# Swin block on one core: a new order of logits, max logits, value blocks and fc2 rows in the attention loop

## The chip, the cores and the metric

The kernel runs on one core of one Trainium2 chip. The metric is the time of one execution on the device, in microseconds (us). Before the change three runs gave 3938.79, 3946.13 and 3956.12 us, median 3946.13 us.

## What is computed

One Swin Transformer block on an image batch x of shape (32, 56, 56, 128), float32, 16 heads of 8 channels, windows of 7 x 7 = 49 tokens, shifted by 3:

```python
y = roll(layernorm(x) * norm1_g + norm1_b, (-3, -3))       # then cut into windows of 49 tokens
q, k, v = split_heads(y @ qkv_w.T + qkv_b)
attn = (q * HD ** -0.5) @ k.T + relative_bias + shift_mask  # 49 x 49 for each window and head
o = softmax(attn) @ v
x = x + roll_back(o @ proj_w.T + proj_b)
h = gelu((layernorm(x) * norm2_g + norm2_b) @ fc1_w.T + fc1_b)   # 512 hidden channels
out = x + h @ fc2_w.T + fc2_b
```

## The kernel before

The work is cut into 128 steps (`STEPS`). A step is a band of 7 image rows of two images: two times 8 windows. A "pair" is the same window of both images, so a step has 8 pairs, w = 0 to 7 (`NW`). One image's tokens lie on partitions 0 to 48 and the other's on 64 to 112. Everything is unrolled in Python: `turns(body)` (L188; each engine has its own `body(t, edge, odd)`) goes over t = -2 to 130, and in turn t an engine works on several steps at once. TensorE's turn t has the transposes, q/k projection and max logits of step t + 1, the logits, exponentials and value products of step t, the projection of step t - 1, fc1 and the last four fc2 rows of step t - 2, and the first three fc2 rows of step t - 3. The order inside a turn is written by hand, one program for each engine; semaphores alone join them. Each engine runs its own program strictly in order.

The softmax needs a maximum for each query and head ahead of the exponentials. It comes from a cheaper product, the "max logits" (high halves of q and k only), computed one turn before: `max_logits` (L743, matmuls L755, 8 for each pair) writes PSUM banks 0 and 1, VectorE's `row_maxima` (L588, reduction L592) takes the maxima, and since there is one such pair of banks, `max_logits` of pair w waits until the maxima of pair w - 1 are taken (`s_max`). For pair 0 it waits for the DMAs that bring its operands mx_k and mx_q (`s_mx_dma`, issued by SyncE at L278 and L282) and for x1 of an earlier step.

`logits` (L766) of pair w has 12 matmuls: the bias and mask by a selection matrix (L785) and q times k with the maximum folded in as a row (L790). It writes banks 2 and 3 for even w and 4 and 5 for odd w, so from w = 2 on it waits for the exponential of pair w - 2 (`s_exp`). ScalarE's `exp_pair` (L404, L411) reads them and writes `probs`, which has four buffers. `pv` (L794, L805) multiplies the probabilities of pairs 2u and 2u + 1 with the values, 64 matmuls into bank 6; it waits for both exponentials, and for ScalarE's copy (`copy_pv`, L414, L419) of the value block before it. ScalarE's order in the loop is exp 0, a copy of v, exp 1, exp 2, copy of block 0, exp 3, exp 4, copy of block 1, exp 5, exp 6, copy of block 2, exp 7; the copy of block 3 opens its next turn.

`fc2` (L823; L837 high parts, L842 low part, 12 matmuls) computes one of the seven image rows of the second MLP product into bank 7. Rows 3 to 6 stand in the attention loop (p = 1), rows 0 to 2 (p = 0) near the start of the turn. VectorE's `finish` (L566, L574) adds the residual; row 0 of the next group waits for it.

After the loop the next turn of TensorE begins with value block 3 (`pv(t - 1, NU - 1)`), the transposes of z2 (L858) and x_in (L866), the transposes of the maxima (L763), fc2 rows 0 to 2 of step t - 3, two chunks of fc1 (L819), the q/k projection (L887), two more chunks of fc1, the spread of the reciprocals (L901), v (L915) and the output projection (L924).

SyncE's queue issues nearly all DMAs, in a fixed order of its own in each turn: `sums` out of `pv_sb`, after the copy of value block 3 (L235, L237); `x_in` (L244, issued at L186), after the x transposes (L243); `oT_raw` (L250); the maxima (L226); `r_rows` (L263), after GpSimd's `r_lo` (L261, L367); the maxima again; `mx_k` (L278); `mx_q` (L282); the output; and the operands of the logits, `st_k` and `st_q` (L297, L300). GpSimd's `r_lo` comes out of VectorE's reciprocal of `sums` (L633).

Of the kernel before, what the change touches and what calls it, by code (L numbers as in the profile page):

```python
# [18 lines left out]
NW = W // WS  # L19
WT = WS * WS  # L20
BT = NW * WT
NU = NW // 2
# [14 lines left out]
EPS = 1e-5  # L37
HALVES = ((0, 4), (4, 7))
FC2_PARTS = ((0, 3), (3, 7))
HT = WS * TP // 2  # L40
W_SCALE = 64.0
LOW_SCALE = 2048.0
# [7 lines left out]
def swin_block_kernel(nc, x, wqT, wkT, wvT, wvpT, wpT, w1T, w2T, cols, rows, table_k, table_q, ident, eye,  # L50
# [11 lines left out]
    with ctx:  # L62
# [101 lines left out]
        def exists(n):  # L164
            return 0 <= n < STEPS

        def past(n, k):
            return n > k
# [332 lines left out]
        def _(dve):  # L501
# [64 lines left out]
            def finish(n, p, edge):  # L566

                i0, i1 = FC2_PARTS[p]
                if p == 1:
# [150 lines left out]
        def _(pe):  # L720
# [45 lines left out]
            def logits(n, w, edge, par):  # L766
                if w == 0:
                    pe.wait_ge(s_st_dma, N_ST * (n + 1))
                    pe.wait_ge(s_neg_dma, N_NEG * (n + 1))
                    if past(n, 1):  # L770
                        pe.wait_ge(s_gelu, CH * (n - 1) - 1)
                    elif n == 1:
                        pe.wait_ge(s_exp, NW - 1)
                elif w == 1:
                    if past(n, 1):
                        pe.wait_ge(s_gelu, CH * (n - 1))
                    elif n == 1:
                        pe.wait_ge(s_exp, NW)
                else:
                    pe.wait_ge(s_exp, NW * n + w - 1)  # L780
                kind = 2 * edge(n) + (w == NW - 1)
                bank = 2 + 2 * (w % 2)
                for b in range(2):
                    for im in range(2):
                        mm(ps[HP * im:HP * (im + 1), bank + b, 0:HB * WT], eye_k[0:BIAS_ROWS, kind, im, :],  # L785
                           bias[0:BIAS_ROWS, b, :], start=True, stop=False)
                    for g in (2 * b, 2 * b + 1):
                        for im in range(2):
                            span = slice((2 * w + im) * WT, (2 * w + im + 1) * WT)
                            last = mm(group(im, bank, g, EQ * WT), st_k[par][:, g, span], st_q[par][:, :, g, span],  # L790
                                      start=False, stop=(g % 2 == 1))
                last.then_inc(s_st, 1)

            def pv(n, u):  # L794
                pe.wait_ge(s_exp, NW * n + 2 * u + 2)
                if u == 0:
                    pe.wait_ge(s_vown, n + 1)
                    pe.wait_ge(s_vown_b, 3 * (n + 1))
                else:
                    pe.wait_ge(s_pv_sb, NU * n + u)  # L800
                for w in (2 * u, 2 * u + 1):
                    for h in range(NH):
                        g, r = h // NR, h % NR
                        first = (2 * g + w % 2) * WT
                        last = mm(ps[32 * r:32 * r + VC, 6, first:first + WT],  # L805
                                  v_own[0:KP, w, h, :], probs[0:KP, w % 4, h * WT:(h + 1) * WT], start=True, stop=True)
                last.then_inc(s_pv, 1)
# [15 lines left out]
            def fc2(n, p, i):  # L823
                first, end = FC2_PARTS[p]
                if i == first and p == 1:
# [18 lines left out]
                    last.then_inc(s_fc2, 1)  # L844

            def body(t, edge, odd):
                if exists(t - 1):
                    pv(t - 1, NU - 1)
                n = t - 2
                if exists(n):  # L850

                    pe.wait_ge(s_z2, n + 1)
                    if exists(t - 1):
                        pe.wait_ge(s_exp, NW * t - 1)
                    else:
                        pe.wait_ge(s_gelu, CH * n)
                    for i in range(WS):
                        last = nc.tensor.transpose(tokens_of(2)[:, i, 0:TP], z2[:, i, :], idn[0:TP, 0:TP])  # L858
                    last.then_inc(s_t2, 1)
                n = t + 1  # L860
                if exists(n):
                    pe.wait_ge(s_z1, n + 1)
                    if past(n, 0):
                        pe.wait_ge(s_max, NW * n)
                    for i in range(WS):
                        last = nc.tensor.transpose(tokens_of(0)[:, i, 0:TP], x_in[odd(1)][:, i, :], idn[0:TP, 0:TP])  # L866
                    last.then_inc(s_t1, 1)
                if exists(t):
                    max_transposed(t)
                if exists(t - 3):  # L870
                    for i in range(*FC2_PARTS[0]):
                        fc2(t - 3, 0, i)
                if exists(t - 2):
                    fc1(t - 2, 0)
                    fc1(t - 2, 1)
                n = t + 1
                if exists(n):
                    pe.wait_ge(s_y_lo, n + 1)
                    high, low = ([y[odd(1)][:, :, im, 0:WT] for im in range(2)] for y in (yT_hi, yT_lo))
                    for w_hi, w_lo, bank in ((wk_hi, wk_lo, 0), (wq_hi, wq_lo, 6)):  # L880
                        if bank == 6 and exists(t):
                            pe.wait_ge(s_negT, t + 1)
                        if bank == 6 and exists(t - 3):
                            pe.wait_ge(s_fin, 2 * (t - 3) + 2)
                        for k, (ww, yy) in enumerate(((w_hi, high), (w_hi, low), (w_lo, high))):
                            for im in range(2):
                                last = mm(ps[:, bank + im, 0:BT], ww[:, :], yy[im], start=(k == 0), stop=(k == 2))  # L887
                        last.then_inc(s_qk, 1)
                if exists(t - 2):
                    fc1(t - 2, 2)  # L890
                    fc1(t - 2, 3)
                n = t - 1
                if exists(n):

                    pe.wait_ge(s_rr_dma, N_RR * (n + 1))
                    if exists(t + 1):
                        pe.wait_ge(s_lo, 2 * (t + 1) + 1)
                    elif not exists(t):
                        pe.wait_ge(s_x1, 2 * n)
                    for b in range(2):  # L900
                        last = mm(tokens_of(0)[:, 4 * b:4 * b + 4, 0:2 * WT], sel[:, :], r_rows[:, 4 * b:4 * b + 4, :],  # L901
                                  start=True, stop=True)
                    last.then_inc(s_spread, 1)
                n = t
                if exists(n):
                    if exists(t + 1):
                        pe.wait_ge(s_lo, 2 * (t + 2))
                    else:
                        pe.wait_ge(s_negT, t + 1)
                        if exists(t - 3):  # L910
                            pe.wait_ge(s_fin, 2 * (t - 3) + 2)
                    for b in range(2):
                        for w in range(4 * b, 4 * b + 4):
                            for part, (yy, ww) in enumerate(((yT_hi, wv_hi), (yT_lo, wv_hi), (yT_hi, wv_lo))):
                                last = mm(ps[:, 7 - b, (w % 4) * C:(w % 4 + 1) * C],  # L915
                                          yy[odd(0)][:, w, :, :].rearrange("p m q -> p (m q)"), ww[:, :],
                                          start=(part == 0), stop=(part == 2))
                        last.then_inc(s_v, 1)
                n = t - 1
                if exists(n):  # L920
                    pe.wait_ge(s_oT, n + 1)
                    for i0, i1 in HALVES:
                        for i in range(i0, i1):
                            last = mm(tokens_of(0)[0:TP, i, :], oT[:, i, :], w_p[:, :], start=True, stop=True)  # L924
                        last.then_inc(s_proj, 1)
                for w in range(NW):
                    if exists(t):
                        if w != 1:
                            logits(t, w, edge, odd(0))
                        if w == 0:  # L930
                            logits(t, 1, edge, odd(0))
                        if w % 2 == 0 and w > 0:
                            pv(t, w // 2 - 1)
                    if exists(t - 2) and w % 2:
                        fc2(t - 2, 1, FC2_PARTS[1][0] + w // 2)
                    if exists(t + 1):
                        max_logits(t + 1, w, edge)

            turns(body)


# [60 lines left out]
```

## Time and profile before

| | before |
|---|---|
| median of three runs | 3946.13 us (3938.79 to 3956.12) |
| the profiled execution | 3954.99 us, span 3953.2 us, mean granted TensorE clock 0.996 |
| busy share of the span | PE 95%, PE weight loads 75%, DVE 78%, ACT 70%, POOL 73% |
| matmuls | 75664 |
| HBM traffic | 106.14 MB read, 51.46 MB written |

PE is TensorE, PEld its weight loads, DVE is VectorE, ACT ScalarE, POOL GpSimd, SP SyncE and SPq its DMA queue. A matmul's start is recorded; its end is modelled, and matmuls overlap, so that a distance from start to start says more than a duration. An idle time in the list of waits counts from the modelled end of the instruction before.

### The profile page before, as it was taken

To read this page: it belongs to the slowest core of one execution; us is meant where nothing else is said; L and a number is where in the kernel's file an instruction comes from. 1 tells how busy PE (TensorE), PEld (TensorE's weight loads), DVE (VectorE), ACT (ScalarE), POOL (GpSimd) and SP (SyncE) were. 2 spreads that over 40 slices of the span, in tenths; PEclk is the share of its full clock that TensorE was granted. 3 is DMA by queue.
4 is the path that set the end of the run, shared out by engine and by line. 5 is a ranking of instruction groups with operands and counts; after the bars stand their busy time and mean duration, and the time that the engine had idled before them with its cause. 6 is when DMAs were issued, how large, how long until landed. Compare 5 with 4: busy or idle time off the path is not lost. (4 is left out here: it accounts for less than half of the span.)

```text
span 3953.2 us, 177003 instructions
## 1 busy us (share of the span) xinstructions
PE 3758.8 (95%) x75664; PEld 2946.1 (75%) x75664; DVE 3089.6 (78%) x7840; ACT 2778.9 (70%) x3840; POOL 2895.7 (73%) x3988
## 2 busy tenths in 40 slices
PE   2899999999999999999999999999999999999997
PEld 1677777777777777777777777777777777777776
DVE  6787788788788778777778878878878877777774
ACT  1677777777777777777777777777777777776674
POOL 5577777777777777777777777777777777777775
PEclk9999999999999999999999999999999999999999
DMA  2333343333333433333434433343343343333331
GB/s 78 105 114 110 117 117 113 117 115 115 117 115 113 118 110 115 118 113 114 117 112 117 115 114 114 112 119 111 114 121 111 115 119 112 113 115 109 110 108 58
DMA packets 609604, 442.02 MB, mean 112 GB/s; under 512 B 142083, under 2 KB 608371, under 8 KB 608819
## 3 DMA queue, kind: packets, MB, share of 16 engines
q1 hardware_dynamic: 608355, 428.88, 36.7%
q8 instruction: 597, 9.78, 1.1%
q0 software_dynamic: 464, 1.81, 0.1%
q14 instruction: 188, 1.54, 0.1%
HBM read 106.14 MB, written 51.46 MB: 40 GB/s over the span
## 5 line engine op out<-in xcount | busy, mean ns | idle before, releaser
L592 DVE TENSOR_REDUCE neg_max<-ps 113x16 f32<-113x784 f32 x1024 | 999.9, 977 | 594.1 <-PE ps L755 443.7
L411 ACT ACTIVATE probs<-ps 113x784 f32<-113x784 f32 x1024 | 849.2, 829 | 704.4 <-PE ps L790 539.7
L380 POOL TENSOR_TENSOR hid_lo<-probs,hid_hi 128x784 f16<-128x784 f32 x512 | 881.6, 1744 | 75.2 <-DVE hid_hi L585 75.0
L790 PE MATMUL ps<-st_q,st_k 128*49 128x196 f16 x8192 | 695.0, 249 | 0.0
L785 PE MATMUL ps<-bias,eye_k 106*64 106x392 f16 x4096 | 684.7, 332 | 0.3 <-issue 0.3
L755 PE MATMUL ps<-mx_k,mx_q 128*49 128x196 f16 x8192 | 544.6, 254 | 93.4 <-DVE neg_max L592 51.6
L790 PEld LDWEIGHTS ps<-st_q,st_k 128*49 128x49 f16 x8192 | 439.8, 105 | 126.4 <-issue 1.3
L426 ACT ACTIVATE probs<-ps,col 128x784 f32<-128x784 f32 x512 | 468.1, 914 | 89.1 <-PE ps L819 59.9
L837 PE MATMUL ps<-w_hi,hid_hi 128*112 128x128 f16 x3584 | 522.2, 226 | 3.8 <-DVE hid_hi L585 3.0
L837 PE MATMUL ps<-w_lo,hid_hi 128*112 128x128 f16 x3584 | 499.5, 220 | 0.0
L837 PEld LDWEIGHTS ps<-w_hi,hid_hi 128*112 128x112 f16 x3584 | 418.1, 130 | 84.1 <-issue 79.7
L805 PE MATMUL ps<-probs,v_own 113*32 113x49 f32 x32768 | 468.7, 209 | 8.0 <-issue 7.3
L805 PEld LDWEIGHTS ps<-probs,v_own 113*32 113x32 f32 x32768 | 396.2, 110 | 91.2 <-issue 89.2
L755 PEld LDWEIGHTS ps<-mx_k,mx_q 128*49 128x49 f16 x8192 | 313.9, 103 | 185.7 <-DVE neg_max L592 73.2
L355 POOL TENSOR_TENSOR x_res<-x_res,proj_b 112x896 f32<-112x896 f32 x128 | 269.0, 2101 | 230.9 <-DMA x_res<-in_x 230.9
L837 PEld LDWEIGHTS ps<-w_lo,hid_hi 128*112 128x112 f16 x3584 | 419.6, 131 | 0.0
L343 POOL TENSOR_SCALAR x_in<-x_in,rs,nm 112x128 f32<-112x128 f32 x896 | 393.2, 455 | 13.5 <-POOL nm L338 0.3
L343 POOL TENSOR_SCALAR z<-x,rs,nm 112x128 f32<-112x128 f32 x896 | 392.2, 454 | 13.5 <-POOL nm L338 0.3
L334 POOL TENSOR_TENSOR rs<-ve,half 112x7 f32<-112x7 f32 x256 | 381.0, 1488 | 21.4
L419 ACT ACTIVATE pv_sb<-ps 128x392 f32<-128x392 f32 x512 | 255.7, 499 | 179.3 <-PE ps L805 168.8
L842 PE MATMUL ps<-w_hi,hid_lo 128*112 128x128 f16 x3584 | 349.4, 220 | 3.5 <-POOL hid_lo L380 3.5
L402 ACT ACT_TABLE_LOAD x253 | 324.6, 1283 | 4.5
(119 smaller groups left out, 7730.2 us busy)
## 6 DMA issues: line engine op xcount, KB each, us to landing
st_k<-k_hi SPq DMA_DIRECT2D x256, 196.0 KB
st_q<-q_hi SPq DMA_DIRECT2D x1024, 49.0 KB
oT_raw<-pv_sb SPq DMA_DIRECT2D x256, 196.0 KB, 3.5
x_in<-in_x SPq DMA_DIRECT2D x224, 196.0 KB
x_res<-in_x SPq DMA_DIRECT2D x224, 196.0 KB
out_y<-y_out SPq DMA_DIRECT2D x224, 196.0 KB
mx_k<-k_hi SPq DMA_DIRECT2D x512, 49.0 KB
mx_q<-q_hi SPq DMA_DIRECT2D x128, 196.0 KB
```

Source lines behind the costliest of these rows:

```text
L334: nc.gpsimd.tensor_tensor(rs[:, :], ve[:, :], half[:, :], ALU.pow).then_inc(s_rs, 1)
L343: last = nc.gpsimd.tensor_scalar(z[:, i, :], src[:, i, :], rs[:, i:i + 1], nm[:, i:i + 1], ALU.mult, ALU.add)
L380: nc.gpsimd.tensor_tensor(hid_lo[:, c, :], hid[:, c, :], hid_hi[:, c, :], ALU.subtract).then_inc(s_hid_lo, 1)
L411: nc.scalar.activation(probs[0:KP, w % 4, :].rearrange("p (b c) -> p b c", b=2), ps[0:KP, b:b + 2, 0:HB * WT], ACT.Exp).then_inc(s_exp, 1)
L426: nc.scalar.activation(hid[:, c, :].rearrange("p (b q) -> p b q", b=2), ps[:, bank:bank + 2, 0:HT], ACT.Gelu, bias=col[:, BF + c:BF + c + ...
L592: nc.vector.tensor_reduce(neg_max[0:KP, :, :, w].rearrange("p e g -> p g e"), ps[0:KP, 0:2, :].rearrange("p b (g c) -> p (b g) c", g=2)[:, ...
L755: last = mm(group(im, 0, g, 256), mx_q[edge(n)][:, g, span], mx_k[:, g, :, span], start=True, stop=True)
L785: mm(ps[HP * im:HP * (im + 1), bank + b, 0:HB * WT], eye_k[0:BIAS_ROWS, kind, im, :], bias[0:BIAS_ROWS, b, :], start=True, stop=False)
L790: last = mm(group(im, bank, g, EQ * WT), st_k[par][:, g, span], st_q[par][:, :, g, span], start=False, stop=(g % 2 == 1))
L805: last = mm(ps[32 * r:32 * r + VC, 6, first:first + WT], v_own[0:KP, w, h, :], probs[0:KP, w % 4, h * WT:(h + 1) * WT], start=True, stop=True)
L837: mm(row, hid_hi[:, c, i * TP:(i + 1) * TP], w_part[:, c, :], start=(c == 0 and w_part is w2_hi), stop=False)
L842: last = mm(row, hid_lo[:, c, i * TP:(i + 1) * TP], w2_hi[:, c, :], start=False, stop=(c == CH - 1))
```

## The change

On TensorE alone, and there in the attention loop of a turn. The logits of pairs 0 and 1 stand ahead of the loop. Inside it pair w's place has, in this order, the max logits of pair w, an fc2 row or a value block, and the logits of pair w + 2 (before: the logits of pair w, a value block or an fc2 row, the max logits of pair w). fc2 rows come behind the max logits of pairs 0, 2, 4 and 7, value blocks behind those of pairs 1, 3, 5 and 6. So value block 3, which opened the next turn, stands behind the max logits of pair 6 and ahead of those of pair 7, and the last fc2 row closes the loop.

```diff
+FC2_AFTER = (0, 2, 4, 7)
+PV_AFTER = (1, 3, 5, 6)
...
             def body(t, edge, odd):
-                if exists(t - 1):
-                    pv(t - 1, NU - 1)
                 n = t - 2
...
+                if exists(t):
+                    logits(t, 0, edge, odd(0))
+                    logits(t, 1, edge, odd(0))
                 for w in range(NW):
-                    if exists(t):
-                        if w != 1:
-                            logits(t, w, edge, odd(0))
-                        if w == 0:
-                            logits(t, 1, edge, odd(0))
-                        if w % 2 == 0 and w > 0:
-                            pv(t, w // 2 - 1)
-                    if exists(t - 2) and w % 2:
-                        fc2(t - 2, 1, FC2_PARTS[1][0] + w // 2)
                     if exists(t + 1):
                         max_logits(t + 1, w, edge)
+                    if exists(t - 2) and w in FC2_AFTER:
+                        fc2(t - 2, 1, FC2_PARTS[1][0] + FC2_AFTER.index(w))
+                    if exists(t) and w in PV_AFTER:
+                        pv(t, PV_AFTER.index(w))
+                    if exists(t) and w + 2 < NW:
+                        logits(t, w + 2, edge, odd(0))
```

## Rows read from the trace of the kernel before

**Rows 1.** The page, part 1: busy time, share of the span, instructions.

```profile
PE 3758.8 (95%) x75664; PEld 2946.1 (75%) x75664; DVE 3089.6 (78%) x7840; ACT 2778.9 (70%) x3840; POOL 2895.7 (73%) x3988
```

**Rows 2.** Waits, whole run: engine, line, releaser; total us, times, longest.

```profile
PE ps L755 <- DVE neg_max L592: 51.6, 137, 1.1
PE ps L755 <- DMA mx_q<-q_hi: 37.1, 42, 4.3
...
PEld ps L755 <- DMA mx_q<-q_hi: 57.7, 70, 5.0
```

**Rows 3.** Time line of PE, end of one loop: start us, us, engine, line, operation.

```profile
2042.38 0.90 PE L805 MATMUL ps<-probs,v_own 113*32 113x49 f32 x64
2043.21 0.53 PE L755 MATMUL ps<-mx_k,mx_q 128*49 128x196 f16 x8
2043.57 0.33 PE L785 MATMUL ps<-bias,eye_k 106*64 106x392 f16 x2
...
2044.36 0.26 PE L837 MATMUL ps<-w_hi,hid_hi 128*112 128x128 f16 x1
...
2044.85 0.39 PE L842 MATMUL ps<-w_hi,hid_lo 128*112 128x128 f16 x4
2045.16 0.53 PE L755 MATMUL ps<-mx_k,mx_q 128*49 128x196 f16 x8
2045.62 0.90 PE L805 MATMUL ps<-probs,v_own 113*32 113x49 f32 x64
2046.45 0.89 PE L858 MATMUL ps<-idn,z 112*128 112x112 f32 x7
2047.18 0.83 PE L866 MATMUL ps<-idn,x_in 112*128 112x112 f32 x7
```

**Rows 4.** Time line of all engines, head of the loop of the same turn.

```profile
2031.72 0.53 PE L755 MATMUL ps<-mx_k,mx_q 128*49 128x196 f16 x8 [0.42 <-DMA mx_q<-q_hi]
...
2032.18 0.26 PE L837 MATMUL ps<-w_hi,hid_hi 128*112 128x128 f16 x1
...
2032.36 0.98 DVE L592 TENSOR_REDUCE neg_max<-ps 113x16 f32<-113x784 f32 x1 [1.46 <-issue]
...
2032.43 0.87 ACT L411 ACTIVATE probs<-ps 113x784 f32<-113x784 f32 x1
...
2033.39 0.53 PE L755 MATMUL ps<-mx_k,mx_q 128*49 128x196 f16 x8 [0.33 <-DVE neg_max L592]
```

**Rows 5.** Time line of PE, a turn without a wait at M0: L1, M0.

```profile
2150.88 0.33 PE L785 MATMUL ps<-bias,eye_k 106*64 106x392 f16 x2
...
2151.57 0.51 PE L755 MATMUL ps<-mx_k,mx_q 128*49 128x196 f16 x8
```

**Rows 6.** Time line of ACT, end of the loop of rows 3.

```profile
2043.35 0.50 ACT L419 ACTIVATE pv_sb<-ps 128x392 f32<-128x392 f32 x1
2044.53 0.82 ACT L411 ACTIVATE probs<-ps 113x784 f32<-113x784 f32 x1 [0.68 <-PE ps L790]
```

**Rows 7.** Time line of DVE there: the maxima of pair 7.

```profile
2045.73 0.98 DVE L592 TENSOR_REDUCE neg_max<-ps 113x16 f32<-113x784 f32 x1 [0.39 <-PE ps L755]
```

**Rows 8.** Time line of SyncE's DMA queue, the turn that follows.

```profile
2047.16 1.24 SPq L237 DMA_DIRECT2D sums<-pv_sb  x2
2048.50 0.97 SPq L186 DMA_DIRECT2D x_in<-in_x  x2
...
2053.58 0.62 SPq L263 DMA_DIRECT2D r_rows<-r_hi  x1
...
2059.22 0.61 SPq L282 DMA_DIRECT2D mx_q<-q_hi  x1
```

**Rows 9.** Waits of SyncE's queue, whole run.

```profile
SPq L261 <- POOL r_lo L367: 33.0, 59, 2.7
SPq L243 <- PE ps L866: 29.0, 7, 18.5
```

**Rows 10.** Time line of POOL, the turn of rows 8: r_lo.

```profile
2052.12 0.29 POOL L367 TENSOR_SCALAR r_lo<-sums 128x98 f16<-128x98 f32 x1
```

## The prediction

> Blocks of TensorE's order in one turn are named here by letter: L0 to L7 the logits of the eight pairs, M0 to M7 the max logits of the next step, F0 to F3 the four fc2 rows, P0 to P3 the four value blocks, z and x the two sets of transposes that open the next turn. A "block length" is the distance from the first matmul of a block to the first of the next.
>
> **What bounds the kernel now.** The page's first part comes first: PE is busy for 95% of the span, the next engine for 78% [rows 1]. So the order on TensorE is the clock, and only what makes TensorE stand can be won or lost. The list of waits says where it stands: in front of the max logits, for the maxima of the pair before (51.6 us in 137 waits) and for the DMA of mx_q (37.1 us in 42; 57.7 us in 70 by the weight loads) [rows 2]. With some 127 full turns that is about 0.4 and between 0.3 and 0.45 us a turn. The time lines then say which block stands. From M2 on nothing does: in [rows 3] P2, M6, L7, F3, M7, P3, z follow each other in 0.83, 0.36, 0.79, 0.80, 0.46, 0.83 and 0.73 us, which is what the same blocks take elsewhere. So the rounds from pair 2 on are already full, and logits that run further ahead of the exponentials can win nothing there. The two waits are at M0 and M1, both at the head of the loop [rows 4].
>
> **The change part by part, in us a turn.** Old order from the head: L0 L1 M0 F0 M1 L2 P0 M2 L3 F1 M3 L4 P1 M4 L5 F2 M5 L6 P2 M6 L7 F3 M7 P3 | z. New: L0 L1 M0 F0 L2 M1 P0 L3 M2 F1 L4 M3 P1 L5 M4 F2 L6 M5 P2 L7 M6 P3 M7 F3 | z. The blocks and their instructions are the same; only places change, and no DMA, VectorE, ScalarE or GpSimd instruction moves in its own queue.
>
> *M1, a gain.* M1 may start when the maxima of M0 are taken. M0 starts at 2031.72, its reduction at 2032.36 and takes 0.98, M1 comes at 2033.39: 1.67 after M0 [rows 4]. In between stand only M0 (0.46) and F0 (0.80, taken from F3, since F0 runs into this wait) [rows 3, 4], 1.26. The wait is 1.67 - 1.26 = 0.41. Now L2 stands there too: a logits block ahead of max logits has length 0.69 [rows 5]. 1.26 + 0.69 = 1.95 is more than 1.67: **-0.41**, all of it. What takes over as cover is enough: P0 then comes 2.41 after M0, and its exp of pair 1 ends 1.58 after M0 (2032.43 + 0.87 against 2031.72) [rows 4]. The waits of L(w+2) on exp(w) have between them the same set of blocks as before (one value block or fc2 row, two of M, one L), so cost nothing.
>
> *P3, a loss.* P3 needs the exponentials of pair 7. L7 starts at 2043.57, exp 7 at 2044.53 and takes 0.82 [rows 3, 6], so it is done 1.78 after the start of L7, and a waiting TensorE block starts some 0.05 later, as M1 does behind its reduction [rows 4]: 1.83. Before, F3 and M7 stood between (0.79 + 0.80 + 0.46 = 2.05), which hid it by 0.2. Now only M6 does: 0.69 + 0.46 = 1.15 [rows 3, 5]. The wait is **+0.68**. Behind it in TensorE's queue are M7, F3 and the next turn, so it is paid in full. ScalarE doesn't make it longer: the copy of P2 starts 0.97 after P2 and takes 0.50 [rows 3, 6]; with P2 0.83 ahead of L7 it ends 0.64 after L7's start, before exp 7 could start (0.96). Next in line: M7 waits for the maxima of M6, 0.69 + 1.67 = 2.36 after L7; it comes at 1.83 + 0.83 = 2.66, no wait. x waits for the maxima of M7 (0.57 + 0.98 = 1.55 after M7 [rows 3, 7]); it comes 0.46 + 0.75 + 0.73 = 1.94 after it, no wait, by 0.4.
>
> *Changes between kinds of tile.* M in front of P takes 0.46, in front of L 0.36 [rows 3]: going from the 49-column tiles to another kind costs 0.10. The last fc2 matmul starts at 2045.02 (four from 2044.85, 0.06 apart) and M7 0.14 later. Before, F3 went into M7 and P3 into z; now P3 goes into M7 and F3, in full-width tiles, into z, also full-width. The trace doesn't show F into z. Bounds: nothing won, or all of 0.14 above zero distance. I take **-0.05**, near the 0.06 at which full-width matmuls follow each other but with something for fp16 to fp32. F into L and P into L aren't shown either; I cost them as F and P into M (0.80, 0.83), since L's tiles lie in the same halves of the columns; either side by 0.03 for six of them is the bound (0.2).
>
> The Trainium skill (TensorEngine Tiling (Array Packing), Key Properties) says that a change of tiling mode drains the engine. By that rule the count decides: 16 changes from M0 to z before, 15 after, one drain less; at the row's 0.10 that gives -0.10 where I take -0.05, and the sum below would be 6 us lower. The trace agrees that M into P costs more than M into L.
>
> *The DMA queue of SyncE.* P3's copy releases the sums DMAs, the first of a row of issues that stand back to back: sums at 2047.16, x_in at 2048.50, then oT, maxima, r_rows at 2053.58, mx_q at 2059.22 [rows 8]. x_in itself needs only the x transposes, which end near 2048.01 [rows 3]; in the whole run the queue stood for them 7 times [rows 9]. Now P3 stands 0.83 + 0.46 + 0.75 = 2.04 ahead of z where it stood 0.83 ahead, so sums goes out 1.2 earlier and x_in at about 2048.10: the row moves up by up to 0.40. It doesn't all arrive: r_rows also waits for GpSimd's r_lo, in 59 of the turns the last to come [rows 9], and r_lo hangs on VectorE's own order (in this turn it ends at 2052.41, 1.17 ahead of r_rows, so here all 0.40 arrives) [rows 8, 10]. 70 turns wait for mx_q at M0 [rows 2]. In those I give 0.25 each, between the 0.40 and what r_lo cuts: 70 x 0.25 / 127 = **-0.14**. Bounds: 0, when the slow issues are limited by transfers, and -0.40, the whole wait.
>
> **Sum:** -0.41 + 0.68 - 0.05 - 0.14 = +0.08 a turn, times 127 turns = +10 us. The profiled execution took 3954.99 us (span 3953.2), 9 us over the median of the three runs, 3946.13, so it is a fair specimen of them; it would become 3965, the median 3956. A measurement of this kernel tells some 0.5% (20 us) from no change, so this is "the same".
>
> **The rivals.**
> 1. *The exp wait at P3 is not repaid: slower.* Place: ahead of P3; price 0.68 against the 0.41 of M1. If SyncE's shift is swallowed by the transfers or r_lo, and F into z costs as F into M, +0.27 x 127 = +34 us, 3980. For it: both numbers come from rows with almost no scatter; against it: x_in is plainly held up by sums. It passes the 20 us bound from a net of 0.16 a turn, that is when the gains of queue and tile change together stay under 0.11.
> 2. *The queue was the real bound: faster.* The mx_q wait goes entirely (-0.40) and F into z is free (-0.14): 0.68 - 0.41 - 0.54 = -0.27, -34 us, 3912. For it: the issues behind sums run without a pause. Against it: r_lo is last in 59 turns. Half of this (-20 us, 3926) is already outside "the same".
> 3. *The new neighbours cost more.* F into L and P into L at the upper bound: +0.2 on the sum, 0.28 x 127 = +36, 3982. Little speaks for it.
> That running ahead does nothing by itself in the full rounds is part of the forecast, not a rival.
>
> **How the numbers follow.** Forecast as it stands 0.55 (within 0.5%); rival 1 0.22; rival 2 0.17; rival 3 0.06. Slower by over 0.5%: 0.22 + 0.06 = 0.28; faster by over 0.5%: 0.17; within: 0.55. The range takes in rivals 1 and 3 with some us above (3985) and half of rival 2 (3925), and leaves out the rest of it.
>
> **What would show it.** Right: M1 stops waiting for the maxima (its 51.6 us nearly gone), and a new wait of about 0.68 x 128 = 87 us, P <- exp, is the longest on PE, behind an L7 to P3 of 1.83. The wait for mx_q falls from 37.1 by 10 to 25 us, and SyncE stands for x (L866) in most turns and not in 7. F3 to z of about 0.75. Wrong: P3 starting 1.15 behind L7 (then the kernel is far faster), any wait at L2 to L7 or P0 to P2, a block length of F or P in front of L above 0.83, or a wait for mx_q as long as before.

## The result and the profile after

The changed kernel takes 3954.92 us, median of 20 runs (3947.13 to 3962.96), against 3946.62 us for the kernel before (20 runs, 3938.79 to 3956.12): a ratio of 1.0021, 95% interval [1.0014, 1.0028], so 8 us more: a loss of 0.2% that is clear of the noise and inside what the prediction called "the same". The forecast was 3956. The two profiled executions are single draws, 3955 us before and 3951 us after, one above and one below its median; so what follows compares parts of a turn and not the spans.

The line numbers of TensorE's helpers went up by two. The list of waits of the changed kernel, TensorE and its weight loads (total us, times, longest), against [rows 2]:

```profile
PEld ps L807 <- ACT probs L413: 116.6, 163, 1.2
PE ps L807 <- ACT probs L413: 82.0, 128, 1.0
...
PEld ps L757 <- DMA mx_q<-q_hi: 44.1, 48, 5.4
...
PE ps L757 <- DMA mx_q<-q_hi: 32.1, 36, 5.0
...
PE ps L757 <- DVE neg_max L594: 9.8, 13, 1.1
```

The wait for the maxima fell from 51.6 us in 137 to 9.8 in 13 and the one for mx_q from 37.1 to 32.1 (57.7 to 44.1 on the weight loads). The 13 that are left all lie in the first turns (68 to 137 us from the start), none in a full turn. A new one leads: 128 waits, 82.0 us, a value block on exponentials. It was 0.7 us before. The head of the loop on TensorE, M0, L2, M1, P0, in a turn of the changed kernel:

```profile
2025.29 0.53 PE L757 MATMUL ps<-mx_k,mx_q 128*49 128x196 f16 x8 [0.98 <-DMA mx_q<-q_hi]
...
2026.56 0.36 PE L787 MATMUL ps<-bias,eye_k 106*64 106x392 f16 x2
...
2027.27 0.51 PE L757 MATMUL ps<-mx_k,mx_q 128*49 128x196 f16 x8
2027.70 0.90 PE L807 MATMUL ps<-probs,v_own 113*32 113x49 f32 x64
```

M1 comes 1.98 after M0 with no wait in front. The end of the loop, L7, M6, P3, M7, F3, z, x, against [rows 3]:

```profile
2036.40 0.36 PE L787 MATMUL ps<-bias,eye_k 106*64 106x392 f16 x2
...
2037.11 0.51 PE L757 MATMUL ps<-mx_k,mx_q 128*49 128x196 f16 x8
2038.25 0.90 PE L807 MATMUL ps<-probs,v_own 113*32 113x49 f32 x64 [0.64 <-ACT probs L413]
2039.08 0.53 PE L757 MATMUL ps<-mx_k,mx_q 128*49 128x196 f16 x8
2039.54 0.26 PE L839 MATMUL ps<-w_hi,hid_hi 128*112 128x128 f16 x1
...
2040.26 0.84 PE L858 MATMUL ps<-idn,z 112*128 112x112 f32 x7
2040.93 0.83 PE L866 MATMUL ps<-idn,x_in 112*128 112x112 f32 x7
```

And ScalarE there, the copy of block 2 and exp 7, against [rows 6]:

```profile
2036.54 0.50 ACT L421 ACTIVATE pv_sb<-ps 128x392 f32<-128x392 f32 x1 [0.31 <-PE ps L807]
2037.38 0.82 ACT L413 ACTIVATE probs<-ps 113x784 f32<-113x784 f32 x1 [0.34 <-PE ps L792]
```

P3 starts 1.85 behind L7, 0.05 after exp 7 ends (2038.20). The copy, done at 2037.04, is no part of it, as worked out. SyncE's queue in the next turn (z at 2040.26), against [rows 8]:

```profile
2039.79 1.25 SPq L239 DMA_DIRECT2D sums<-pv_sb  x2
2041.85 0.81 SPq L188 DMA_DIRECT2D x_in<-in_x  x2
...
2046.23 0.62 SPq L265 DMA_DIRECT2D r_rows<-r_hi  x1
...
2051.86 0.61 SPq L284 DMA_DIRECT2D mx_q<-q_hi  x1
```

with its waits over the run, against [rows 9]:

```profile
SPq L245 <- PE ps L866: 124.5, 126, 18.9
SPq L263 <- POOL r_lo L369: 50.6, 63, 2.6
```

sums now goes out before z, and x_in waits for the x transposes in 126 turns where it did in 7: x_in goes out 1.59 behind the start of z instead of 2.05.

### The profile page after: what moved, and what is told of

It is laid out like the page before. It is cut to its first block, busy times and chain, and to the rows that moved or that the text cites. A ratio compares the mean times of both kernels' runs of the same rounds, so it can differ in the third digit from the quotient of the medians.

```text
span 3949.7 us, 177003 instructions
## 1 busy us (share of the span) xinstructions
PE 3732.6 (95%) x75664; PEld 2941.4 (74%) x75664; DVE 3082.5 (78%) x7840; ACT 2781.5 (70%) x3840; POOL 2885.2 (73%) x3988
## 4 chain that ended last, share of the span: by engine, by line
PE 78%; SPq 9%; DMA 3%; ACT 3%; issue 2%; DVE 1%; POOL 1%; ACTq 0%; POOLq 0%; DVEq 0%
PE ps L807 11%; PE ps L839 11%; PE ps L787 10%; PE ps L821 9%; PE ps L792 8%; PE ps L757 8%; PE ps L887 4%; PE ps L844 4%; PE ps L924 4%; DMA mx_q<-q_hi 3%; PE ps L915 3%; SPq L280 3%; ACT probs L413 3%; PE ps L858 2%; SPq L228 2%; PE ps L866 2%
## 5 line engine op out<-in xcount | busy, mean ns | idle before, releaser
L787 PE MATMUL ps<-bias,eye_k 106*64 106x392 f16 x4096 | 704.2, 340 | 0.0
L757 PE MATMUL ps<-mx_k,mx_q 128*49 128x196 f16 x8192 | 528.7, 250 | 44.4 <-DMA mx_q<-q_hi 32.1
L757 PEld LDWEIGHTS ps<-mx_k,mx_q 128*49 128x49 f16 x8192 | 362.0, 103 | 69.4 <-DMA mx_q<-q_hi 44.1
```

The costliest lines, as they stand in the source:

```text
L757: last = mm(group(im, 0, g, 256), mx_q[edge(n)][:, g, span], mx_k[:, g, :, span], start=True, stop=True)
```

## The experiments

TensorE's starts were compared block by block over the full turns of each trace (124 in most); "a turn" below is a mean over them. Every ratio is to the kernel before, run beside it on the same chip. There are three such groups, and the kernel before took 3949.06 us in the first (the changed kernel again, the sums DMAs held back, the fc2 row, the head alone), 3953.94 in the second (the changed kernel again, x_in in both kernels, the block cut in two) and 3946.82 in the third (the last two runs). So times are compared within a group, and ratios across groups.

**The changed kernel again**, as the measure for the runs beside it.

> The changed kernel again, as the measure for the runs beside it on the same chip. Both theories: +8 us over the kernel before, 1.002, as measured.

1.0015 [1.0006, 1.0025], 3954.51 us. In the second group:

> The changed kernel again, as the measure for the runs beside it on the same chip: +8 us over the kernel before.

1.0020 [1.0011, 1.0029], 3962.00 us.

**The sums DMAs held back**, the rest as in the changed kernel:

```diff
                     sp.wait_ge(s_pv_sb, NU * (n + 1))
+                    if exists(t - 2):
+                        sp.wait_ge(s_t2, t - 1)
                     for im in range(2):
                         sp.dma_start(sums[:, im, :], ...)
```

> The changed kernel, but SyncE issues the sums DMAs only after the z transposes (it waits for s_t2), so they go out about 0.9 us after the start of z, as late as in the kernel before (0.7) or a little later. Nothing moves on TensorE. Theory A (two waits on TensorE changed places, and SyncE's queue gives a part back): the wait for mx_q at M0 returns from 0.28 us a turn to 0.40 or somewhat more, +0.15 to +0.25 a turn, +20 to +30 us over the changed kernel, 3975 to 3985. Rival B (the queue's earlier start gave nothing, what was won lies in the tile changes): no change, 3955.

3982.34 us, 1.0090 [1.0077, 1.0104]: 28 us over the changed kernel beside it, and this with TensorE's order untouched. Waits of this kernel:

```profile
PEld ps L759 <- DMA mx_q<-q_hi: 65.8, 83, 5.0
...
PE ps L759 <- DMA mx_q<-q_hi: 43.4, 57, 4.3
```

Against the first trace of the changed kernel the wait at M0 went from 32.1 to 43.4 us (44.1 to 65.8 on the weight loads) and TensorE's wait for r_rows from 1.9 to 9.2. Block by block against the changed kernel beside it, a turn loses 0.15 at M0 and 0.05 in front of the spread matmuls, 26 of the 28 us. So the earlier start of SyncE's row is worth real time, and rival B falls. Held back to 0.93 behind z, it goes out 0.2 later than in the kernel before, so the 28 us are an upper figure for what the change won there.

**The fc2 row between M6 and P3:**

```diff
-FC2_AFTER = (0, 2, 4, 7)
+FC2_AFTER = (0, 2, 4, 6)
```

> The changed kernel with the last fc2 row moved between M6 and P3 (order L7 M6 F3 P3 M7, then z). Theory A: L7 to P3 is 0.71 + 0.44 + 0.81 = 1.96, over the 1.83 that exp 7 takes, so the 0.70 wait at P3 is gone; but x now stands 0.46 + 0.73 = 1.19 behind M7 and the maxima of M7 take 1.60, a new wait of 0.41 at x; tile changes cost 0.15 more. Net -0.14 a turn, -18 us against the changed kernel, 3937. Rival B (the waits inside the loop are swallowed at M0 by the mx_q wait): no change, 3955. Rival D (the new wait at x doesn't come): -70 us.

3957.70 us, 1.0024 [1.0015, 1.0033]: 3 us over the changed kernel, where theory A expected 18 less. TensorE, M6, F3, P3, M7, z, x:

```profile
2044.27 0.51 PE L757 MATMUL ps<-mx_k,mx_q 128*49 128x196 f16 x8
2044.70 0.26 PE L839 MATMUL ps<-w_hi,hid_hi 128*112 128x128 f16 x1
...
2045.51 0.90 PE L807 MATMUL ps<-probs,v_own 113*32 113x49 f32 x64
2046.34 0.53 PE L757 MATMUL ps<-mx_k,mx_q 128*49 128x196 f16 x8
2046.80 0.89 PE L858 MATMUL ps<-idn,z 112*128 112x112 f32 x7
2048.03 0.67 PE L866 MATMUL ps<-idn,x_in 112*128 112x112 f32 x5 [0.34 <-DVE neg_max L594]
```

and the maxima of pair 7 on VectorE:

```profile
2046.91 0.98 DVE L594 TENSOR_REDUCE neg_max<-ps 113x16 f32<-113x784 f32 x1 [0.54 <-PE ps L757]
```

The wait at P3 is gone and the one at x is there, as theory A has it, so rival D falls. It is larger: z to x takes 1.23 and not 0.73, a wait of 0.50 instead of 0.41. The maxima are ready at 2047.89 and x starts 0.14 later, not the 0.05 seen in front of max logits. That is 0.09 of the 0.17 a turn by which the forecast missed. The other 0.08 lies between P3 and M7 (mean 0.97, in the changed kernel beside it 0.89; the median is 0.83 in both): in some turns TensorE stops for about a microsecond inside the value block. The last section comes back to these stops. So the exponentials' wait of 0.70 was turned into 0.50 for the maxima, 0.15 of tile changes and 0.08 of stops.

**The head alone**, in the kernel before:

```diff
-                        if w != 1:
+                        if w not in (1, 2):
                             logits(t, w, edge, odd(0))
...
                         fc2(t - 2, 1, FC2_PARTS[1][0] + w // 2)
+                    if exists(t) and w == 1:
+                        logits(t, 2, edge, odd(0))
```

> The kernel before with one thing of the change alone: the logits of pair 2 stand ahead of M1, all else in the old order (L0 L1 M0 F0 L2 M1 P0 M2 L3 F1 M3 ...). Theory A: the 0.40 wait at M1 is gone, but M1 to M2 now has only M1 and P0 between, 0.44 + 0.83 = 1.27 against the 1.67 that maxima take, so the same 0.40 stands at M2: no change against the kernel before, 3947. Rival (the gain at the head is there for itself and the tail's new order is pure loss): -0.40 a turn, -51 us, 3896.

3931.74 us, 0.9962 [0.9950, 0.9975]: 17 us less. Both expectations miss. TensorE, M0, L2, M1, P0, M2:

```profile
2050.97 0.53 PE L755 MATMUL ps<-mx_k,mx_q 128*49 128x196 f16 x8 [0.16 <-DMA mx_q<-q_hi]
...
2052.23 0.36 PE L785 MATMUL ps<-bias,eye_k 106*64 106x392 f16 x2
...
2052.94 0.51 PE L755 MATMUL ps<-mx_k,mx_q 128*49 128x196 f16 x8
2053.38 0.90 PE L805 MATMUL ps<-probs,v_own 113*32 113x49 f32 x64
2054.52 0.53 PE L755 MATMUL ps<-mx_k,mx_q 128*49 128x196 f16 x8 [0.24 <-DVE neg_max L592]
```

The wait did move to M2, but is 0.31 there (P0 to M2 1.14 instead of 0.83) and not 0.40: from M1 to M2 the maxima take 1.58, from M0 to M1 1.67. The chain is shorter because the reduction starts 0.55 behind M1 where it starts 0.63 behind M0. Summed over M0 to L3, the block lengths give 0.11 less a turn in the mean (0.08 by the medians), 13 of the 17 us, and the interval spans 11 us. What follows for the change: moving the one block keeps three quarters of the wait, at M2. To be rid of it the later max logits need a logits block more in front of them too, as the whole change gives them. Even so this one move is faster than the whole change (0.9962 against 1.0015), since it leaves P3 its cover.

**x_in behind mx_q in SyncE's queue**, in both kernels; the block is moved whole to the place ahead of the output DMAs:

```diff
-                n = t + 3
-                if exists(n):
-                    ...
-                    band_dmas(sp, xr, x_in[odd(3)], n, edge(n), False, s_x)
...
                         dst mx_q, src q_hi
+                n = t + 3
+                if exists(n):
+                    ...
+                    band_dmas(sp, xr, x_in[odd(3)], n, edge(n), False, s_x)
```

> The kernel before with SyncE's x_in DMAs moved from in front of oT_raw to behind mx_q; nothing moves on TensorE. Theory A (mx_q comes late because x_in's issue, 1.0 to 2.4 us, stands ahead of it in the queue): r_rows is then held by r_lo alone, mx_q goes out some 0.4 us earlier in the mean, and the wait at M0 falls from 0.40 to about 0.1 a turn: -0.3 x 127 = -38 us, 3908. Rival C (transfers, not issues, hold mx_q up): no change, 3947.

3937.58 us, 0.9961 [0.9946, 0.9976], some 16 us less and not 38. Little of it is at M0: against the trace of the kernel before, a turn is 0.135 shorter, or 17 us, of which M0 has 3. Some 10 us are the stops inside blocks at the turn's start: 13 of them with 11.0 us in the kernel before, one with 0.5 us here. SyncE's row now stands for r_lo in 125 turns (153.2 us) where it did in 59, so mx_q's issue moves up by 0.29 and no more.

> The changed kernel with the same move of x_in behind mx_q. Theory A: the wait at M0 falls from 0.28 to about 0.1: -0.18 x 127 = -23 us against the changed kernel, 3932; and since the queue no longer counts in either, the change by itself then costs more than its 8 us, some 20 to 25 us over the kernel before with the same move. Rival B (queue gave nothing): the difference between the two stays 8 us.

3954.88 us, 1.0003 [0.9994, 1.0012]: 7 us under the changed kernel beside it and not 23. The direction is theory A's: without x_in in the way the change costs 1.0003 against 0.9961, 17 us (expected 20 to 25), and not 8; the two intervals leave some 7 us either way. The gain from mx_q is far smaller than expected, and the turns say why. mx_q goes out 12.18 us behind z before, 11.89 in the changed kernel, 11.89 and 11.77 in these two; the wait at M0 is 0.40, 0.28, 0.37 and 0.27 a turn. So going out earlier takes only short waits away: those where M0 starts up to 3.2 us behind mx_q's issue fall from 19.1 to 10.8 us in the kernel before, the longer ones go from 30.1 to 35.5. What is left is taken up in the last section.

**The last value block cut in two:** the half for pair 6 behind M6, then F3, M7, the half for pair 7. `pv` gets an argument `half`, waits for one exponential less in the first half, and signals in the second only.

```diff
-                    if exists(t - 2) and w in FC2_AFTER:
-                        fc2(t - 2, 1, FC2_PARTS[1][0] + FC2_AFTER.index(w))
-                    if exists(t) and w in PV_AFTER:
-                        pv(t, PV_AFTER.index(w))
+                    if exists(t) and w in (1, 3, 5):
+                        pv(t, w // 2)
+                    if exists(t) and w == 6:
+                        pv(t, NU - 1, 0)
+                    if exists(t - 2) and w in (0, 2, 4, 6):
+                        fc2(t - 2, 1, FC2_PARTS[1][0] + w // 2)
+                    if exists(t) and w == 7:
+                        pv(t, NU - 1, 1)
```

> The changed kernel with value block 3 cut in two: its half for pair 6 behind M6, then fc2 row 3, M7, its half for pair 7, z. Theory A: L7 to the second half is far over 1.83, so no wait for exp 7; M6 to M7 is 0.44 + 0.42 + 0.81 = 1.67, just the time of the maxima; M7 to x is 0.46 + 0.42 + 0.73 = 1.61, just enough. So neither the wait of the old kernel at M1 nor that of the new one at P3 stands anywhere; one more change between kinds of tile (0.14); SyncE's queue as in the kernel before. -0.28 a turn against the changed kernel, 3919, and 28 us under the kernel before. Rival B (waits in the loop are swallowed at M0): no change, 3955.

3920.22 us, 0.9920 [0.9905, 0.9936]. The 3919 expected was for a chip on which the kernel before takes 3947; here it takes 3954, so the gain is larger than forecast: 34 us under the kernel before (expected 28) and 42 under the changed kernel beside it (expected 36). TensorE, L7, M6, first half, F3, M7, second half, z, x:

```profile
2055.32 0.36 PE L787 MATMUL ps<-bias,eye_k 106*64 106x392 f16 x2
...
2056.03 0.51 PE L757 MATMUL ps<-mx_k,mx_q 128*49 128x196 f16 x8
2056.47 0.56 PE L807 MATMUL ps<-probs,v_own 113*32 113x49 f32 x32
2056.95 0.26 PE L840 MATMUL ps<-w_hi,hid_hi 128*112 128x128 f16 x1
...
2057.76 0.53 PE L757 MATMUL ps<-mx_k,mx_q 128*49 128x196 f16 x8
2058.21 0.56 PE L807 MATMUL ps<-probs,v_own 113*32 113x49 f32 x32
2058.70 0.89 PE L859 MATMUL ps<-idn,z 112*128 112x112 f32 x7
2059.45 0.86 PE L867 MATMUL ps<-idn,x_in 112*128 112x112 f32 x7
```

No wait stands in the loop behind M0. Against the changed kernel it is 1.0% faster (0.9920 to 1.0020): that is the price of the wait at P3, shown by taking it away, less one more change of tile kind and the queue's part (the wait at M0 is 0.36 here and 0.30 in the changed kernel beside it). This excludes that waits in the loop are swallowed at M0.

**Both together**, with the cut kernel again beside it.

> The kernel with the last value block cut in two again, as the measure for the run beside it: 0.992 of the kernel before, as measured.

0.9932 [0.9919, 0.9946], 3917.91 us.

> Both: value block 3 cut in two, and x_in's DMAs behind mx_q in SyncE's queue. Theory A, corrected by the runs so far (issuing mx_q earlier takes away only the short waits at M0; those where the transfers land over 3.2 us after their issue, 25 of 124 turns with 30 of the 49 us, stay): the two gains add, 0.992 x 0.996 = 0.988 of the kernel before, 3903 to 3910; the wait at M0 stays near 0.3 a turn. Rival: both gains are the same turns' waits, so it stays at 0.992.

3909.50 us, 0.9903 [0.9888, 0.9919]. This is the fastest version: 37 us (1.0%) under the kernel before, at the upper end of the expected 3903 to 3910 and a little over the expected 0.988. Against the cut kernel beside it, it wins 8 us, and the two intervals touch. So of the 16 us that the late x_in won in the kernel before about half adds. The wait at M0 is 0.37 a turn, as long as in the cut kernel (0.35), and not 0.3. The stops inside blocks fit this: the cut kernel has only 2 of them, so there is little to win there.

## Why the prediction was right, point by point

The time (3956 against 3955) and the class were right. The two waits that decide it were right in mechanism and size; that the time was hit within 1 us is partly luck, since the tile term was taken at a third of what it is. By terms, in us a turn, forecast and then measured between the two traces:

| term | forecast | measured |
|---|---|---|
| wait at M1 | -0.41 | -0.40 |
| wait at P3 | +0.68 | +0.70 |
| changes between kinds of tile | -0.05 | -0.14 |
| SyncE's queue | -0.14 | -0.15 (M0 -0.11, the spread matmuls -0.04) |
| sum | +0.08 | +0.01; by the medians of the runs 8.3 / 127 = +0.07 |

*The two waits* were right in place and size. Both chains (max logits, reduction, next max logits; logits, exponential, value block) hardly scatter: from M6 to P3 it takes 1.14 in nearly every turn where the blocks alone take 0.44. The cut block confirms the size on the other side, the head alone that M1's gain isn't there for itself.

*The tile term* was mis-sized. F3 into z takes 0.71, not 0.75, and z to x 0.68, not 0.73; with the 0.05 of the forecast that makes 0.14. F and P in front of L cost what they cost in front of M (0.81, 0.83), as assumed. A logits block behind an fc2 row or a value block is 0.02 longer than assumed (0.71 for 0.69) and a max logits block behind logits 0.02 shorter (0.44 for 0.46), six of each, which cancels. The rule weighed there (the Trainium skill, TensorEngine Tiling (Array Packing), Key Properties: a change of mode drains the engine) gave -0.10 by its count of one change less, nearer to the measured -0.14 than my -0.05. The trace agrees with it: F3 takes 0.71 into the full-width z and 0.81 into the 49-column max logits, 0.10 for the change.

*The queue term* was right in sign and size, and held by the sums DMAs held back (+28 us). The reason I gave for its limit, r_lo, was half of it: r_lo came last in 63 turns, but the larger limit is how long mx_q takes to land. One sign was missed: TensorE's wait for mx_q in the list was to fall by 10 to 25 us and fell by 5.0 (37.1 to 32.1); only counted by starts, weight loads included, is it 14 (49 to 36).

*The rest:* the measured terms add up to 0.06 a turn less than the medians show. One trace of each kernel can't settle this: that of the kernel before lies 8 us above its median, 0.07 a turn, so it isn't the fair specimen that the prediction took it for, and that of the changed kernel 3 below. The wait at M0 is 0.28, 0.31 and 0.30 in the three traces of the changed kernel. Nor did the prediction have a term for the stops inside blocks, since the one turn that it read shows none: over the full turns P3 to z takes 0.93 in the mean and not 0.83. They are 13 with 11.0 us in the trace before and 6 to 8 with 5.5 to 8.1 us in the three of the changed kernel. Rival 1 needed the gains of queue and tile change to stay under 0.11 together; they are 0.29. Rival 2 failed on M0, where 0.28 of 0.40 stayed. Rival 3 had no case. That logits further ahead win nothing in the full rounds held: no wait stands at L2 to L7 before or after.

## What to carry to other kernels

Where an engine is full, write down for each chain between engines the time from block to block that it needs, and count which blocks stand in between: a new order is good when every chain has its cover at once. Here the change covered the maxima at the head and uncovered the last exponentials, 0.40 for 0.70, and was nearly saved by two side effects, the earlier start of a DMA row and one change of tile kind less. Cutting one block in two made the filler that was missing, and won 0.8%. Of the orders of whole blocks only the smallest move, one logits block at the head, won anything (0.4%); the full one lost 0.2%.

## What the runs showed of the hardware that was not expected

The long waits at M0 don't come from a late issue. Of 124 turns of the kernel before 76 wait there, 49 us in all; in 25 of them M0 starts over 3.2 us behind mx_q's issue, and these hold 30 of the 49 us. In every one of the 25 a packet of an instruction load (16 KB on one DMA engine, 0.9 to 1.7 us) lies between the issues of mx_k and M0; in the 48 turns without a wait that is so in 20. In the changed kernel it is 22 of 22 with 26 us, and over all twelve traces 287 of 291, against 286 of the 713 turns without a wait. Two windows of the changed kernel that begin less than 0.1 us ahead of mx_q's issue, GB/s in 40 slices and the queue's packets; first a turn where M0 started 3.70 behind the issue (2021.59 to 2025.29):

```profile
GB/s 149 248 33 0 0 0 172 182 149 132 0 0 0 0 231 314 380 347 396 248 83 0 17 17 0 17 0 17 0 17 162 184 249 216 210 183 167 167 156 151
...
q8 instruction: 1, 0.02, 2.2%
```

The stream of some 300 GB/s ends half way through the window, and then single packets at 17 GB/s drip for 0.8 us, as if one engine had its share left behind the instruction packet. Then a turn where M0 didn't wait (mx_q at 2051.86, M0 at 2054.75):

```profile
GB/s 231 165 17 0 0 0 66 182 231 50 0 0 0 50 281 396 330 297 330 357 261 210 156 221 183 189 178 146 146 151 151 162 173 226 232 281 341 325 391 304
```

Here the stream runs on into the next transfers. That the instruction packet is the cause is argued from this coincidence; no run moved the packets, so it isn't shown. It would explain why mx_q issued earlier won less than its share.

TensorE also stops in the middle of a block, mostly in P3. In the kernel before, the last value block of a turn, where the wait ends with nothing that the profile shows:

```profile
317.35 0.75 PE L805 MATMUL ps<-probs,v_own 113*32 113x49 f32 x49
319.17 0.38 PE L805 MATMUL ps<-probs,v_own 113*32 113x49 f32 x15 [1.07 <-issue]
```

The semaphores were taken before the first of the 64 matmuls, and other blocks of this kind take 0.83. There are 85 such stops (over 0.5 us between two matmuls of one block of P, z, x, M or F) in the full turns of the twelve traces, and each of the 85 ends 1.2 to 1.7 us after a 16 KB instruction packet ended; of moments spread over the 3 us from P3's start on, 12% lie so. That TensorE waits there for its next instructions is the likely reading. It is argued from this coincidence, and from the run that moved x_in's DMAs away from the turn's start, which left one stop of 13.
